# A ring of gathered rows with 24 slots instead of 32, in a two-layer graph network on one core

## The chip, the cores and the metric

The kernel runs on one core of a Trainium2 chip. The metric is the device time of one execution in microseconds (us). TensorE is called PE below, VectorE DVE, ScalarE ACT, GpSimd POOL and SyncE SP, as the profile does.

## The reference

The graph has 3125 nodes with 128 features and 53125 directed edges, sorted by their target node. The first network is three relational convolutions, the second a sum over neighbours with a small network behind it:

```python
def rgcn_conv(x, edge_index, edge_type, W, root, bias):
    out = x @ root + bias
    for r in range(8):
        mask = edge_type == r
        h = x @ W[r]
        msg = jnp.where(mask[:, None], h[src], 0)
        agg = segment_sum(msg, dst, N)
        cnt = segment_sum(mask, dst, N)
        out = out + agg / jnp.maximum(cnt, 1.0)[:, None]
    return out

h = relu(layernorm(x))
for W, root, b in three layers:
    h = relu(rgcn_conv(h, (src, dst), edge_type_8, W, root, b))
x = x + h
h = relu(layernorm(x))
h = h + segment_sum(h[src], dst, N)
h = relu(h @ W1 + b1) @ W2 + b2
x = x + batchnorm(h) * gamma + beta
```

## The kernel before

The edges are cut into 416 tiles of 128. A layer first makes a table in HBM: for each node its row times each of the eight relation matrices (`transform`, L512, on PE; `evacuate`, L742, on ACT and DVE; `store_rows`, L1073, on SP). Then, tile by tile, POOL gathers the 128 rows that a tile's edges name with one indirect DMA (`gather`, L1232, issued at L1234; the first 11 tiles of layers 1 and 2 at L1254, with their own indices). DVE writes a selection matrix of 128 by 64 for the tile (`select`, L946, the instruction at L958), which holds one over the edge count at each edge's target. PE multiplies the two and adds to the sums of a group of nodes in PSUM (`sum_tile`, L543, the matmul at L556). When the last tile of a group is summed, ACT closes it (`close_rel`, L750, the instruction at L752) and PE transforms its nodes for the next table.

There are three such layers (0, 1 and 2), so 1248 tiles in a row. The first 48 tiles of layer 0 (`FORE`) are gathered from the input instead, before the first table is ready (L1225), and don't use the ring. The other 1200 go through the ring `rows` of `SLOTS` slots. In what follows a **batch** is eight tiles (`BATCH`), counted from 0 at tile 48: layer 0 holds batches 0 to 45, layer 1 batches 46 to 97, layer 2 batches 98 to 149. The last tile of each layer comes by other DMAs, from SP (`fetch_ends`, L1088).

Beside the sums each layer has other work. In layer 0 DVE counts the edges of each key (L936, two instructions per tile). In layer 1 the neighbour matrix of the second network is built in 416 steps, one per tile, through all three engines: ACT makes a one-hot block (L840, L846), PE multiplies (`pairs`, L637), DVE adds it in place (`add`, L1046, the instruction at L1054). In layer 2 PE multiplies with that matrix (L663). At tile 12 of layers 1 and 2 (`LATE_SUM`) PE also runs `late_sums` (L601): 64 matmuls at L611 for the two last blocks of nodes, whose rows the first 11 gathers leave out.

The order on each engine is written out by hand, and engines meet at semaphores. Three rings tie the engines together:

- `rows`, `SLOTS` slots: POOL waits before each batch until PE has summed the batch that last used the slots. PE counts whole batches in `s_mm`.
- `sel`, 32 slots: DVE waits in the same way, also on `s_mm`, before each batch.
- each slot of `rows` has its own semaphore `s_row`, by which a gather tells PE that it has landed.

POOL's loop is this (L1247 to L1250):

```python
G = TILES * L + t
if G % BATCH == 0 and G >= FORE + SLOTS:
    pool.wait_ge(s_mm, (G + BATCH - SLOTS - FORE) // BATCH)
```

With 32 slots batch j waits until batches 0 to j-4 are summed. The space of `rows` is also used for some intermediate values before the first gather (L330 to L338), which need 2615 of its columns per partition.

Of the kernel before, what the change touches and what calls it, by code (L numbers as in the profile page):

```python
# [29 lines left out]
STEP = 7  # L30
EARLY = 32
HALO = 64
SLOTS = 32
BATCH = 8
SELS = 32
CHUNK = 16
# [51 lines left out]
def gnn_kernel(nc, x, src_t, dst_t, type_t, limits, w_rel, root_w, bias_w,  # L88
# [31 lines left out]
    def pieces(L, t):  # L120

        s, found = start_of[t], []
        for k, (b0, b1) in enumerate(span_of[L]):
            lo, hi = max(s, P * b0), min(s + SPAN, P * b1)
            if lo < hi:
                found.append((k, lo - P * b0, lo - s, hi - lo))
        return found
# [72 lines left out]
    def gathered(G):  # L200

        return sum(1 for g in range(FORE + (G - FORE) % SLOTS, G + 1, SLOTS) if g not in END_TILES)

# [17 lines left out]
    with ExitStack() as ctx:  # L221
        def sb(name, shape, dt=F32):
            return ctx.enter_context(nc.sbuf_tensor(name, shape, dt))

        def sem(name):
            return ctx.enter_context(nc.semaphore(name))

        x_rows = sb("x_rows", [P, BLOCKS, D])
        xT = sb("xT", [P, NP])
        rows = sb("rows", [P, SLOTS, D])  # L230
        sel = sb("sel", [P, SELS, SPAN])
# [175 lines left out]
        s_xT = sem("s_xT")  # L407
        s_row = [sem(f"s_row{n}") for n in range(SLOTS)]
        s_sel = sem("s_sel")
# [133 lines left out]
        def sum_tile(pe, L, t):  # L543
# [6 lines left out]
            else:  # L550
                pe.wait_ge(s_row[G % SLOTS], 16 * gathered(G))
                mine, edges = rows[:, G % SLOTS, :], slice(0, P)
            for k, at, in_window, width in pieces(L, t):
# [550 lines left out]
        def wait_table(pool, L):  # L1104
            if L == GIN:
                pool.wait_ge(s_xr_out, 16 * SUMS[LAST_REL])
                return
            for n in range(ALL_STAGES):
                pool.wait_ge(s_stage[n], 32 * stores_of(n, BLOCKS * (L + 1)))
# [101 lines left out]
        def _(pool):  # L1211
# [25 lines left out]
            with pool.If(fast != 0):  # L1237
                for L in range(GIN):
# [6 lines left out]
                    for t in range(0 if L else FORE, TILES):  # L1245
                        G = TILES * L + t
                        if L and t == LATE_TILES:  # L1247
                            wait_table(pool, L)
                        if G % BATCH == 0 and G >= FORE + SLOTS:
                            pool.wait_ge(s_mm, (G + BATCH - SLOTS - FORE) // BATCH)  # L1250
# [546 lines left out]
```

## Time and profile before

| | |
|---|---|
| median of three runs | 2008.41 us |
| all three | 2002.71, 2008.41, 2010.31 us |
| profiled execution, span from first to last instruction | 2002.7 us |
| profiled execution, its own time | 2002.71 us (the first of the three above: nothing lies around the span) |
| POOL busy | 1189.5 us, 59% |
| PE busy, matmuls | 1093.9 us, 55% |
| PE weight loads | 801.0 us, 40% |
| DVE busy | 848.6 us, 42% |
| ACT busy | 636.3 us, 32% |

A busy share says how long the engine's instructions are shown to run. POOL's instructions here are issues of indirect DMAs: what is shown is POOL's own part of them, not the transfer. "Idle before" in a row is the time that the engine sat idle before the instructions of the row; behind the arrow stands what ended it: "issue" is idle time with no wait that the profile shows, "remote" a semaphore whose writer the profile can't name.

### The profile page before, as it was taken

Reading aid. Unit: us, or ns where it says so; the run is one execution under the profiler, and the core shown is the slowest. Engines: PE = TensorE matmul, PEld = TensorE weight load, DVE = VectorE, ACT = ScalarE, POOL = GpSimd, SP = SyncE. Lnnn points to the kernel's source line nnn. Section 1 sums busy time; section 2 is a strip of 40 time slices with the busy share of each in tenths; the row PEclk is TensorE's granted clock in tenths of the full one; section 3 lists DMA queues with packets and bytes.
Section 4 is the critical chain, followed back from the end, with each engine's and each line's share of the span. In section 5 each row is a group of like instructions: output and inputs, shape, how many; then the busy total and the mean of one; then the engine's idle time right before and its main releaser. Section 6 shows DMA issues by size and latency. Waiting matters only on the chain.

```text
span 2002.7 us, 17513 instructions
## 1 busy us (share of the span) xinstructions
PE 1093.9 (55%) x4627; PEld 801.0 (40%) x4627; DVE 848.6 (42%) x3270; ACT 636.3 (32%) x1147; POOL 1189.5 (59%) x1254
## 2 busy tenths in 40 slices
PE   6496663344433454636564635584526445566677
PEld 2155343334333343434343424353524424253454
DVE  3365465565445235645655545562122212221223
ACT  4220410000000236756665656680201111111133
POOL 5445756666666555666566556645666666676650
PEclk8597866565556655656555565665557576666678
DMA  7352323242323311212222121222111111111111
GB/s 220 119 199 61 95 80 111 68 124 78 99 78 89 95 35 41 79 52 60 64 58 70 45 75 43 85 67 59 42 46 49 42 49 46 44 49 45 45 39 34
DMA packets 80801, 144.18 MB, mean 72 GB/s; under 512 B 24687, under 2 KB 38248, under 8 KB 80696
## 3 DMA queue, kind: packets, MB, share of 16 engines
q0 software_dynamic: 39840, 81.67, 15.9%
q1 hardware_dynamic: 40424, 60.68, 8.9%
q8 instruction: 41, 0.67, 0.1%
q10 hardware_dynamic: 432, 0.64, 0.1%
q14 instruction: 64, 0.52, 0.1%
HBM read 100.23 MB, written 42.67 MB: 71 GB/s over the span
## 4 chain that ended last, share of the span: by engine, by line
another core or an unknown queue 27%; PE 25%; issue 23%; DVE 20%; ACT 3%; SPq 1%; DMA 1%; DVEq 1%; ACTq 0%; POOLq 0%
PE ps_agg L556 8%; DVE sel L958 6%; DVE early L1054 5%; DVE agg_s L936 5%; PE ps_h L525 3%; PE ps_a L643 3%; DVE scratch L1043 2%; PE ps_h L663 2%; PE ps_a L663 2%; PE ps_a L574 2%; PE ps_agg L611 1%; PE ps_a L597 1%; ACT w_all L812 1%; PE ps_agg L585 1%
## 5 line engine op out<-in xcount | busy, mean ns | idle before, releaser
L1234 POOL DMA_INDIRECT rows<-h_table,idx x1175 | 1118.1, 952 | 683.3 <-issue 346.9
L556 PEld LDWEIGHTS ps_agg<-sel,rows 128*128 128x128 f32 x2764 | 570.9, 272 | 361.7 <-issue 335.0
L556 PE MATMUL ps_agg<-sel,rows 128*128 128x64 f32 (+14 forms) x2764 | 552.4, 332 | 254.6 <-issue 239.3
L958 DVE TENSOR_SCALAR sel<-iota,early,norm 128x64 f32<-128x64 f32 x1178 | 353.6, 333 | 432.9 <-remote 279.2
L643 PE MATMUL ps_a<-scratch 128*128 128x300 bf16 x416 | 162.0, 390 | 309.4 <-issue 150.0
L1054 DVE TENSOR_TENSOR early<-ps_a,early 128x300 f32 x416 | 195.9, 471 | 317.1 <-remote 254.1
L840 ACT ACTIVATE scratch<-scratch,ones 128x300 bf16<-128x300 f32 x416 | 221.3, 532 | 225.2 <-remote 198.0
L525 PE MATMUL ps_h<-w_all,xT 128*128 128x512 f32 x300 | 202.7, 787 | 111.1 <-issue 38.7
L846 ACT ACTIVATE scratch<-iota,code_lo 128x300 f32<-128x300 f32 x416 | 226.5, 545 | 12.5
L936 DVE TENSOR_SCALAR_CACHE_REDUCE agg_s<-scratch,key_f 128x256 bf16<-128x256 int16 x416 | 193.6, 473 | 50.1 <-issue 41.5
L643 PEld LDWEIGHTS ps_a<-scratch 128*128 128x128 bf16 x416 | 58.2, 140 | 351.0 <-issue 336.0
L1043 DVE TENSOR_SCALAR scratch<-iota,code_lo 128x128 bf16<-128x128 f32 x416 | 129.8, 312 | 0.0
L525 PEld LDWEIGHTS ps_h<-w_all,xT 128*128 128x128 f32 x300 | 63.0, 244 | 151.1 <-issue 73.9
L747 ACT COPY stage<-ps_h 128x512 f32<-128x512 f32 x80 | 46.4, 583 | 183.1 <-remote 111.4
L812 ACT CAST stage<-early 128x3072 bf16<-128x3072 uint8 x13 | 35.7, 2751 | 210.4 <-remote 117.8
L752 ACT ACTIVATE xT<-ps_agg,vecs 128x512 f32<-128x512 f32 (+2 forms) x16 | 9.4, 586 | 284.0 <-remote 246.4
L1225 POOL DMA_INDIRECT early<-x_table,early x48 | 45.9, 956 | 30.3 <-DMA x_table<-early 16.0
L663 PE MATMUL ps_h<-stage,scratch 128*128 128x512 bf16 x108 | 41.5, 496 | 21.5 <-issue 21.2
L812 ACT CAST w_all<-early 128x3072 bf16<-128x3072 uint8 x12 | 32.9, 2749 | 61.2 <-remote 45.4
L759 ACT ACTIVATE hid<-ps_agg,vecs 128x512 f32<-128x512 f32 (+3 forms) x10 | 5.3, 527 | 142.3 <-remote 102.9
L574 PE MATMUL ps_a<-early 128*128 128x384 f32 (+36 forms) x158 | 42.1, 397 | 11.5 <-issue 11.4
L936 DVE DVE_READ_ACCUMULATOR agg_s<-scratch,key_f 128x1 f32 x416 | 34.2, 82 | 31.4 <-issue 31.2
(157 smaller groups left out, 734.8 us busy)
## 6 DMA issues: line engine op xcount, KB each, us to landing
h_table<-stage SPq DMA_DIRECT2D x130, 256.0 KB
rows<-h_table,idx POOLq DMA_INDIRECT x1175
scratch<-key_rows SPq DMA_DIRECT2D x26, 544.0 KB
h_table<-scratch SPq DMA_DIRECT2D x20, 256.0 KB
x_rows<-in_x SPq DMA_DIRECT2D x6, 256.0 KB, 5.8
w_all<-in_W SPq DMA_DIRECT2D x3, 512.0 KB, 6.6
x_table<-early SPq DMA_DIRECT2D x6, 256.0 KB, 2.3
out<-early SPq DMA_DIRECT2D x6, 256.0 KB
```

Of the source, the lines that this page charges most:

```text
L525: nc.tensor.matmul(half_bank(L, b, half)[:], xT[:, block_of(b)], w_all[:, L, 4 * half:4 * half + 4, :].rearrange("p r o -> p (r o)"), star ...
L556: mm = nc.tensor.matmul(sums_of(L, k)[:, at:at + width], mine, sel[edges, G % SELS, in_window:in_window + width], start=False, stop=(t == ...
L643: nc.tensor.matmul(ps_a[a % A_BANKS][:, 0:HOT], low[:, a % HOTS, :], hot[:, a % HOTS, :], start=True, stop=True).then_inc(s_step, 1)
L663: mm = nc.tensor.matmul(ps_out[q][:], xp[:, b, part, :], fill_of(b)[:, WIDE * q:WIDE * q + WIDE], start=(b == 0 and part == 0), stop=False)
L812: nc.scalar.copy(fill_of(b), adjacency[:, b, 0:SPARE]).then_inc(s_fill, 1)
L840: nc.scalar.activation(hot[:, a % HOTS, :], apart[:, a % 2, :], ACT.Relu, bias=ones[:, 0:1], scale=-1.0).then_inc(s_hot, 1)
L846: nc.scalar.activation(apart[:, a % 2, :], iota[:, EARLY:EARLY + HOT], ACT.Abs, bias=code[:, a:a + 1]).then_inc(s_apart, 1)
L936: done = nc.vector.tensor_scalar(match[:, t % BATCH, :], chunks[:, c % 2, at:at + 2 * P], key_f[:, t:t + 1], 0.0, ALU.is_equal, ALU.add, a ...
L958: done = nc.vector.tensor_scalar(mine, here, dst, weight, ALU.is_equal, ALU.mult)
L1043: nc.vector.tensor_scalar(low[:, a % HOTS, :], iota[:, EARLY:EARLY + P], lo_f[:, a:a + 1], None, ALU.is_equal).then_inc(s_low, 1)
L1054: nc.vector.tensor_tensor(mine, ps_a[a % A_BANKS][:, 0:HOT].rearrange("p (b d) -> p b d", d=REACH), mine, ALU.add).then_inc(s_add, 1)
L1234: pool.indirect_dma_start(rows[:, slot, :], None, table, bass.IndirectOffsetOnAxis(ap=column, axis=0)).then_inc(landed, 16)
```

## The change

```diff
-SLOTS = 32
+SLOTS = 24
```

`SLOTS` is read in four places: the size of `rows` (24 slots of 512 bytes per partition, so 3072 columns, still more than the 2615), the number of `s_row` semaphores, the slot and the count that PE waits for in a tile (`G % SLOTS` and `gathered`), and POOL's wait. The wait stays one per batch, but with 24 slots batch j waits until batches 0 to **j-3** are summed, one batch more than before. Gathers, matmuls and all other instructions stay the same and in the same order.

On POOL this shows at one place, behind the wait for the first table, with the engine's waits shown. `s_mm` is the count of summed batches:

```order
 L1234 DMA rows<-h_table,idx 128x128 [waits s_stage3,s_stage2,s_stage4,s_stage1,s_stage0]
-L1234 DMA rows<-h_table,idx 128x128 x31
+L1234 DMA rows<-h_table,idx 128x128 x23
+L1234 DMA rows<-h_table,idx 128x128 [waits s_mm]
+L1234 DMA rows<-h_table,idx 128x128 x7
 L1234 DMA rows<-h_table,idx 128x128 [waits s_mm]
 L1234 DMA rows<-h_table,idx 128x128 x7
```

The first wait on PE comes after 24 gathers instead of 32, and from there on each wait asks for one batch more.

## Rows read from the trace of the kernel before

**Rows 1.** Groups of POOL's instructions: times, busy us, mean ns, idle before.

```profile
L1234 POOL DMA_INDIRECT rows<-h_table,idx x1175 | 1118.1, 952 | 683.3 <-issue 346.9 <-PE ps_agg L556 153.7 <-remote 144.8
```

**Rows 2.** Stretches of the first 48 gathers, busy us and instructions of each engine.

```profile
core 0: us, PE busy (x) PEld busy (x) DVE busy (x) ACT busy (x) POOL busy (x), PEclk, DMA share, GB/s
22.00:38.00 16.00, 15.95 (x44) 7.54 (x43) 4.67 (x6) 8.69 (x15) 12.14 (x13) 0.95 0.76 230
38.00:54.00 16.00, 4.98 (x6) 1.04 (x5) 0.09 (x1) 1.76 (x3) 12.04 (x14) 0.58 0.56 189
90.00:106.00 16.00, 14.51 (x35) 6.41 (x35) 11.97 (x51) 12.82 (x20) 0.00 (x0) 0.94 0.75 267
```

**Rows 3.** Timeline of POOL, layer 0: first gathers of batches 11, 28, 31, 33, 45.

```profile
259.17 1.15 POOL L1234 DMA_INDIRECT rows<-h_table,idx  x1 [7.80 <-PE ps_agg L556]
...
452.97 0.95 POOL L1234 DMA_INDIRECT rows<-h_table,idx  x1 [4.45 <-remote]
454.22 0.95 POOL L1234 DMA_INDIRECT rows<-h_table,idx  x1 [0.30 <-issue]
...
487.10 0.95 POOL L1234 DMA_INDIRECT rows<-h_table,idx  x1 [4.42 <-remote]
...
509.96 0.95 POOL L1234 DMA_INDIRECT rows<-h_table,idx  x1 [3.15 <-remote]
...
646.75 0.94 POOL L1234 DMA_INDIRECT rows<-h_table,idx  x1 [4.48 <-remote]
```

**Rows 4.** Stretches of batches 28 to 30, columns as in Rows 2.

```profile
453.00:467.00 14.00, 12.34 (x52) 11.39 (x52) 11.53 (x55) 0.00 (x0) 10.65 (x12) 0.50 0.32 89
467.00:487.00 20.00, 1.06 (x4) 0.86 (x3) 6.24 (x24) 0.00 (x0) 12.02 (x13) 0.50 0.18 46
```

**Rows 5.** Timeline: the last matmul of a group in layer 0, and ACT's closing.

```profile
374.66 0.17 PE L556 MATMUL ps_agg<-sel,rows 128*128 128x9 f32 x1 [2.42 <-issue]
...
395.95 0.69 ACT L752 ACTIVATE xT<-ps_agg,vecs 128x512 f32<-128x512 f32 x1 [63.68 <-remote]
```

**Rows 6.** Timeline of POOL, layer 1: first gathers of batches 46, 51, 53.

```profile
666.58 0.95 POOL L1254 DMA_INDIRECT rows<-h_table,late  x1 [11.39 <-issue]
...
733.64 0.97 POOL L1234 DMA_INDIRECT rows<-h_table,idx  x1 [17.24 <-PE ps_agg L556]
...
758.91 0.94 POOL L1234 DMA_INDIRECT rows<-h_table,idx  x1 [5.53 <-PE ps_agg L556]
```

**Rows 7.** Stretches at layer 1's start, as in Rows 2; half of `late_sums`, first to last start.

```profile
680.00:700.00 20.00, 2.25 (x9) 1.75 (x9) 2.67 (x9) 3.27 (x6) 15.12 (x17) 0.50 0.20 53
...
716.00:733.50 17.50, 16.82 (x78) 16.30 (x78) 4.10 (x15) 4.88 (x10) 0.39 (x1) 0.50 0.02 6
...
L611 PE MATMUL ps_agg<-w_all,stage x32: 275/402/447, 719.8 to 731.1; 128*128 128x64 f32 x16, 53*128 53x64 f32 x16
```

**Rows 8.** Timeline of POOL, layer 2: tile 11, then batches 103, 119, 146, and tile 414.

```profile
1356.92 0.95 POOL L1234 DMA_INDIRECT rows<-h_table,idx  x1 [2.10 <-issue]
...
1406.45 0.95 POOL L1234 DMA_INDIRECT rows<-h_table,idx  x1 [13.57 <-PE ps_agg L556]
...
1590.40 0.95 POOL L1234 DMA_INDIRECT rows<-h_table,idx  x1 [6.68 <-PE ps_agg L556]
...
1898.94 0.95 POOL L1234 DMA_INDIRECT rows<-h_table,idx  x1 [4.41 <-remote]
...
1942.04 0.94 POOL L1234 DMA_INDIRECT rows<-h_table,idx  x1 [0.30 <-issue]
```

**Rows 9.** The stretch of `late_sums` in layer 2, columns as in Rows 2.

```profile
1371.00:1396.00 25.00, 3.44 (x12) 3.43 (x12) 1.93 (x8) 0.00 (x0) 16.70 (x18) 0.50 0.19 50
```

**Rows 10.** Timeline of POOL, layer 1: first gathers of batches 59, 60, 62.

```profile
832.31 0.95 POOL L1234 DMA_INDIRECT rows<-h_table,idx  x1 [1.98 <-remote]
...
843.95 0.95 POOL L1234 DMA_INDIRECT rows<-h_table,idx  x1 [1.94 <-remote]
...
869.86 0.94 POOL L1234 DMA_INDIRECT rows<-h_table,idx  x1 [6.13 <-PE ps_agg L556]
```

## The prediction

> **What bounds the kernel now.** I read four views in this order: the groups of POOL's instructions, the stretches, POOL's timeline, and PE's and ACT's timelines beside it. In the groups the reader sees POOL, with 1175 of the 1197 ring gathers on one line, busy 1118.1 us, idle 683.3 us before them, and a good half of that "issue" [rows 1]. A gather takes 0.95 us and the next starts 1.25 us after it, so eight seem to take 10.0 us [rows 3]. That isn't the real pace. From batch 11 to batch 45 the starts move by 646.75 - 259.17 = 387.6 us for 34 batches, 11.40 us each: 34.13 us for three (28 to 31), 22.86 us for two (31 to 33) [rows 3]. The pauses of 4.4 us after three batches and 3.15 us after two are what the 1.25 us pace left out. So a gather really costs about 34.13 / 24 = **1.42 us**, and a pause only brings POOL's shown time level with its real time. In layer 2 it is the same: batches 119 to 146 take (1898.94 - 1590.40) / 27 = 11.43 us each [rows 8]. 1197 gathers of 1.42 us are 1700 us of the 2002.7. POOL is the bound of layers 0 and 2, and what it loses outside this are true waits.
>
> The second thing to see is what a long run of gathers does to everyone else. POOL issues its first 48 gathers without a pause from 22 us on. In the first 16 us PE starts 44 matmuls and ACT 15 instructions; in the next 16 us PE starts 6, DVE 1 and ACT 3. After 90 us, when 48 real gathers (68 us) are over, the counts are 35, 51 and 20 again [rows 2]. The same in layer 0: in the 14 us behind the pause at 452.97 PE starts 52 matmuls and DVE 55 instructions, in the 20 us after that 4 and 24, though POOL issues as before; the pause at 487.10 ends it [rows 3, 4]. Signals are late too: the last matmul of a group starts at 374.66, but ACT's closing starts at 395.95, just before POOL's next run [rows 5]. I call this a **slow stretch**. In these rows it begins about 14 to 16 us after POOL's last restart and ends when POOL has to stop and its real work is done. A longer ring lets POOL run on for longer between stops, so it buys rows in advance and pays with slow stretches.
>
> **The change, part by part.** No instruction is added or removed. Batch j now waits for batch j-3 instead of j-4: each stop comes one batch earlier, 8 x 1.42 = 11.4 us of real work.
>
> *Layer 0, start.* POOL truly waits for PE here (7.80 us idle before batch 11 [rows 3]; 1.42 x 8 - 10.0 = 1.4 us of it for each batch run without a pause is only levelling). A slot less asks for a batch that comes up to 11.4 us later, and the slow stretch before it ends up to 11.4 us earlier. I take 0, with both ends, -11.4 and +11.4.
>
> *Layers 0 and 2, steady.* POOL stays at its real pace. PE's rows come up to 11.4 us later, covered by PE's distance behind POOL. If that cover is gone PE waits for each gather, and still POOL sets the pace. What is new is more stops: 11.43 us per batch in runs of two against 11.38 in runs of three; in runs of one it is 843.95 - 832.31 = 11.64 [rows 10]. Over 34 batches in layer 0 and 43 in layer 2 (103 to 146) that is 77 x 0.05 = 4 us if three become two, and 77 x 0.26 = 20 us if all become one. Three became two is what one batch less makes, so +4.
>
> *Layer 0, end.* Batch 46 starts at 666.58 [rows 6], 19.8 us after batch 45, which has seven gathers (its tile 415 comes by SP): 7 x 1.42 = 9.9 us of work and 9.9 us of waiting for the table, whose last transforms PE does in the burst after the slow stretch that ended at 646.75. A slow stretch one batch shorter lets PE reach them earlier, at most by the 9.9 us; nothing makes them later but rows that come late. I take -4, ends -9.9 and 0.
>
> *Layer 1, start.* This is the largest term. POOL runs through batches 46 to 50 (40 gathers) and then waits 17.24 us for batch 47, until 733.64 [rows 6]. In batch 47 lies `late_sums`. Between 680 and 700 PE starts 9 matmuls in 20 us; between 716 and 733.5 it starts 78 in 17.5 us, `late_sums` among them, at the same granted clock of 0.50 (the 1.2 GHz level) [rows 7]. With 24 slots POOL must stop after 24 gathers, at 666.58 + 24 x 1.42 = 700.7, wait for batch 46 (summed by then), and run batch 49 alone before it has to wait for batch 47. From 700.7 on PE finds only 11.4 us of gathers, less than the 14 us at which stretches turned slow. PE had still to do one or two tiles (about 1 us each when quick) before the point it was at by 716: it gets there at 702.3, and finishes batch 47 17.6 us later (733.64 - 716), at 719.9 instead of 733.6: **-13.7**. POOL's batch 51, which now asks for batch 48, is not late by this. Layer 1 behind that point is paced by PE, DVE and ACT, not by POOL's pace (batches 53 to 62 take (869.86 - 758.91) / 9 = 12.3 us each [rows 6, 10]), so I let the gain stand to the layer's end. Within layer 1 each gather batch is released by PE already; released by j-3 instead of j-4 the same pattern runs one batch apart, and I take 0. The ends of the term are 0 (the signal of batch 46 comes late, nothing is won) and -16.
>
> *Layer 2, start.* The same form, but POOL is the bound behind it. From 1356.92 POOL runs 29 gathers, to the end of batch 102, real end 1398.1; PE starts 12 matmuls in the 25 us from 1371 to 1396 [rows 9], and batch 103 waits for batch 99 until 1406.45 [rows 8]. With 24 slots POOL stops after 21 gathers, at 1386.7. PE is quick 11.4 us earlier, less some 1.7 us for what it did in them anyway: batch 99 is done at 1396.7. Batch 102 starts then, 103 at 1408.1: **+1.6**, ends -2 and +11.4 (the full batch, if the slow stretch doesn't shorten). If a stop before 1590.40 then goes away, where POOL truly waits 6.68 - 3 x 1.4 = 2.4 us, that wait is late next and I leave it.
>
> *End.* The last gather starts at 1942.04 [rows 8], 60 us before the end, and PE has over two batches to sum behind it; with a shorter ring it can't be that far behind. Up to -8, taken as 0, since PE's dense work there has to be done in any case.
>
> Sum: 0 + 4 - 4 - 13.7 + 0 + 1.6 + 0 = -12.1 us. It stands against the profiled execution, 2002.7, which is also the fastest of the three; against the median, 2008.4, it gives **1996 us**.
>
> **The rivals.** *A, slower: the lost batch isn't paid back.* Its place is the stop behind which POOL is the bound: the start of layer 0 and batch 103. If slow stretches follow the number of gathers in flight or some clock of their own and don't shorten, each costs the full 11.4 us, 22.8 in all, and the more frequent stops cost 4 to 20 more: 2008.4 + 27 = 2035, up to 2051. It decides from the point at which batch 103 starts later than about 1412 on the clock of before. For it speaks that POOL is the bound; against it the three places [rows 2, 4, 7] where the slowness begins after a run of POOL and ends with it. The Trainium skill's page "DMA: Bandwidth & Descriptors" has in its "Rules for kernel authors" the rule to issue a DMA early and wait on its semaphore late, since its fixed cost is then hidden; by it 32 slots are the better ring, and this rival is what it would do. The trace speaks half against it: beyond about 14 us the early issue slows those who need the rows.
>
> *B, no difference.* The 13.7 us at layer 1's start are given back, because layer 1's pace isn't PE's own but set by the same slow stretches, which there depend on how PE and POOL fall together (11.64 us for one batch, 25.9 for the next two [rows 10]). Then 0 + 4 + 0 + 1.6 - 4 = 2010.
>
> *C, much faster.* The opposite in layer 1: the pattern with its double runs turns into single runs of 11.64. Layer 1's 44 batches from 53 on would win up to 44 x (12.3 - 11.6) = 31 us more: 1965.
>
> That the change does nothing because the ring never fills is excluded: POOL's stops are the ring's stops.
>
> **How the numbers follow.** A measurement of this kernel can tell about 0.5% from no change, here 10 us. My forecast has 0.45, with a range of its own of 1980 to 2010: the bounds of its terms added as if they were independent. B has 0.24, A 0.22, C 0.09. Faster than 1998.4 are two thirds of the forecast's cases, C, and a sixth of B: 0.30 + 0.09 + 0.04, and I give 0.44. Slower than 2018.4 are nearly all of A, a tenth of B and little of the forecast: 0.24. The rest, 0.32, is no difference. The range from 1970 to 2037 leaves out the far half of A and of C, about 0.15 to 0.2.
>
> **What would show it.** POOL's first wait for PE comes after 24 ring gathers, and runs between pauses are mostly of two batches. The pause of 17.24 us in layer 1 becomes two, and PE's `late_sums` there begins some 13 us earlier after the layer's first gather. In layer 2 batch 102, not 103, is the one that waits long, and 103 starts within 3 us of where it did, counted from the layer's first gather. The steady pace stays at 11.4 to 11.5 us per batch. I am wrong if slow stretches begin as early and last as long as before, if the steady pace goes over 11.7, or if layer 1's batches take more than 12.5 us each.

## The result, and the profile after

The changed kernel takes **1986.36 us** (median of 11 runs, 1970.03 to 2004.73), the kernel before, run beside it, 2010.31 us (11 runs, 1999.54 to 2034.9). The ratio is 0.9856, 95% interval [0.9829, 0.9883]: 1.4% faster, some 29 us. It leaves out slow runs, those over 1.5% above their kernel's fastest (three of the changed kernel's eleven), while the medians of all runs are 24 us, 1.2%, apart. Forecast were 1996 us and 0.6%. The time lies in the range, but the gain is at least twice the one forecast, and the sum's largest error has one place, the end of the program.

The page of the changed kernel: span, busy time, and the groups that answer to [rows 1] and to PE's sums.

```profile
span 1980.7 us, 17490 instructions
...
PE 1113.7 (56%) x4604; PEld 815.1 (41%) x4627; DVE 848.9 (43%) x3270; ACT 635.1 (32%) x1147; POOL 1187.1 (60%) x1254
...
L1234 POOL DMA_INDIRECT rows<-h_table,idx x1175 | 1115.8, 950 | 688.7 <-issue 343.3
...
L556 PE MATMUL ps_agg<-sel,rows 128*128 128x64 f32 (+14 forms) x2764 | 582.5, 341 | 255.7 <-issue 193.4
```

Nothing is to be seen in these totals: POOL is as busy and as idle as in [rows 1], within 6 us. The gain must be found in the order of time. POOL's timeline after, where it restarts: a steady stop in layer 0, the first gathers of layer 1 (batch 46), a pause inside batch 47, batch 51, the first gather of layer 2 (batch 98), batch 102, and the last gather.

```profile
333.30 0.94 POOL L1234 DMA_INDIRECT rows<-h_table,idx  x1 [4.75 <-remote]
...
670.38 0.94 POOL L1254 DMA_INDIRECT rows<-h_table,late  x1 [9.38 <-issue]
...
687.15 0.97 POOL L1234 DMA_INDIRECT rows<-h_table,idx  x1 [3.34 <-issue]
...
726.74 0.97 POOL L1234 DMA_INDIRECT rows<-h_table,idx  x1 [13.62 <-PE ps_agg L556]
...
1329.66 0.94 POOL L1254 DMA_INDIRECT rows<-h_table,late  x1 [12.09 <-DMA h_table<-stage]
...
1382.82 0.94 POOL L1234 DMA_INDIRECT rows<-h_table,idx  x1 [10.53 <-PE ps_agg L556]
...
1934.38 0.94 POOL L1234 DMA_INDIRECT rows<-h_table,idx  x1 [0.31 <-issue]
```

Counted from layer 1's first gather, the long wait of layer 1 ends 56.4 us later (726.74 - 670.38), where it was 67.1 us ([rows 6]: 733.64 - 666.58). Both waits are for the same sum, that of batch 47: batch 50 asks for it now, batch 51 did before. The stretches that answer to [rows 2], [rows 7] and [rows 9], and half of `late_sums`:

```profile
core 0: us, PE busy (x) PEld busy (x) DVE busy (x) ACT busy (x) POOL busy (x), PEclk, DMA share, GB/s
...
38.00:54.00 16.00, 5.21 (x6) 1.29 (x6) 0.00 (x0) 1.75 (x3) 12.15 (x13) 0.59 0.56 183
...
684.00:704.00 20.00, 13.35 (x59) 11.89 (x59) 10.10 (x42) 10.32 (x21) 12.88 (x14) 0.63 0.24 67
704.00:727.00 23.00, 11.98 (x54) 11.84 (x55) 4.70 (x16) 5.10 (x10) 7.24 (x9) 0.50 0.10 24
1361.00:1383.00 22.00, 10.63 (x45) 10.11 (x44) 0.41 (x2) 1.84 (x1) 8.73 (x11) 0.50 0.12 31
...
L611 PE MATMUL ps_agg<-w_all,stage x32: 275/401/467, 702.0 to 724.2; 128*128 128x64 f32 x16, 53*128 53x64 f32 x16
```

In layer 1 PE starts 59 matmuls in the 20 us from 684 on, where [rows 7] had 9, and in layer 2 45 in the 22 us up to batch 102's start, where [rows 9] had 12 in 25. `late_sums` starts 31.6 us after the layer's first gather (702.0 - 670.38) instead of 53.2 (719.8 - 666.58), but runs for 22.2 us instead of 11.3, so its head start is not all kept. The slow stretch within the first 48 gathers, which the ring doesn't touch, is unchanged.

The last lines of the sums, by PE's timeline: first the kernel before, then after. The last gather starts at 1942.04 before [rows 8] and at 1934.38 after.

```profile
1968.44 0.43 PE L556 MATMUL ps_agg<-sel,wide 5*128 5x64 f32 x2
```

```profile
1945.20 0.43 PE L556 MATMUL ps_agg<-sel,wide 5*128 5x64 f32 x2
```

PE's last sum followed POOL's last gather by 26 us before and by 11 us now. This **tail** is the part of the gain that the prediction put at nothing.

### The profile page after: what moved, and what is told of

It is laid out like the page before. It is cut to its first block, busy times and chain, and to the rows that moved or that the text cites. A ratio compares the mean times of both kernels' runs of the same rounds, so it can differ in the third digit from the quotient of the medians.

```text
span 1980.7 us, 17490 instructions
## 1 busy us (share of the span) xinstructions
PE 1113.7 (56%) x4604; PEld 815.1 (41%) x4627; DVE 848.9 (43%) x3270; ACT 635.1 (32%) x1147; POOL 1187.1 (60%) x1254
## 4 chain that ended last, share of the span: by engine, by line
issue 23%; PE 20%; POOL 20%; another core or an unknown queue 19%; DVE 12%; ACT 3%; DMA 1%; SPq 1%; DVEq 1%; ACTq 0%; POOLq 0%
POOL rows L1234 20%; PE ps_agg L556 5%; DVE early L1054 5%; PE ps_a L643 3%; DVE sel L958 3%; PE ps_h L525 3%; DVE scratch L1043 2%; PE ps_a L574 2%; PE ps_agg L611 1%; PE ps_a L663 1%; ACT scratch L840 1%; PE ps_h L663 1%; DMA rows<-h_table,idx 1%; PE ps_a L597 1%
## 5 line engine op out<-in xcount | busy, mean ns | idle before, releaser
L556 PEld LDWEIGHTS ps_agg<-sel,rows 128*128 128x128 f32 x2764 | 585.4, 276 | 381.2 <-issue 297.2
L556 PE MATMUL ps_agg<-sel,rows 128*128 128x64 f32 (+14 forms) x2764 | 582.5, 341 | 255.7 <-issue 193.4
L747 DVE COPY stage<-ps_h 128x512 f32<-128x512 f32 x50 | 34.0, 680 | 37.8 <-remote 16.6
```

The costliest lines, as they stand in the source:

```text
L556: mm = nc.tensor.matmul(sums_of(L, k)[:, at:at + width], mine, sel[edges, G % SELS, in_window:in_window + width], start=False, stop=(t == ...
L747: copy(stage_of(H)[:, 512 * half:512 * half + 512], half_bank(L, b, half)[:]).then_inc((s_evA, s_evD)[half], 1)
```

## The experiments

There were eighteen runs, some of them of the same kernel again, in five groups, each group on one chip beside the kernel before. The chips turned out to be of two kinds, and this matters more than any edit. On the one kind (two chips, called **A chips** here, and by its time the chip of the first result) the kernel before takes 2007 and 2012 us; on the other (three chips, **B chips**) it takes 1622 us. Each result below says which kind it is from. "j-3" means that a batch waits for the one three before it.

### The wait alone

32 slots, waits as in the changed kernel:

```diff
-if G % BATCH == 0 and G >= FORE + SLOTS:
-    pool.wait_ge(s_mm, (G + BATCH - SLOTS - FORE) // BATCH)
+if G % BATCH == 0 and G >= FORE + 24:
+    pool.wait_ge(s_mm, (G + BATCH - 24 - FORE) // BATCH)
```

> The ring keeps its 32 slots; only POOL's wait asks for batch j-3 instead of j-4. Theory (a shorter run of gathers gives shorter slow stretches, the slots themselves do nothing): as the changed kernel, ratio to before 0.982 to 0.990, layer 1's long wait for PE split in two, PE's last sum 12 to 20 us earlier. Rival (the smaller ring itself, its addresses or its 8 semaphores fewer, brings the time): 0.997 to 1.003.

A chip: 1983.63 us (1976.76 to 1992.91), ratio 0.9882 [0.9826, 0.9938], the same as the changed kernel within the intervals. It is the wait that brings the gain; the ring's size and its place in memory have no part in it that can be seen.

### One batch less again

The same edit with 16 in place of 24, so j-2.

> 32 slots, but POOL's wait asks for batch j-2, as a ring of 16 would. Theory: nearly every run of gathers is one batch, so slow stretches almost vanish, but now PE lacks rows: a batch takes 11.4 us of gathers and 2.2 us to land, while PE is left with one batch in hand. Layers 0 and 2 stay at 11.6 to 11.8 us per batch (some +20 us against the changed kernel), layer 1 gets 0 to +2 us per batch: 1990 to 2080 us, slower than the changed kernel. Rival (the shorter the run the better): under 1965 us.

A chip: 1969.24 us (1958.42 to 1974.92), ratio 0.9777 [0.972, 0.9834]. I had expected it to be slower or equal, and it is the fastest kernel on this kind of chip. PE's group now says why it isn't better still: its idle time ends mostly with a row that lands, so PE runs right behind the gathers.

```profile
L556 PE MATMUL ps_agg<-sel,rows 128*128 128x64 f32 (+14 forms) x2764 | 656.2, 359 | 291.5 <-DMA rows<-h_table,idx 208.1
```

### Gathers paced by their landing

As before (j-4), but each gather first waits until that two before it has landed:

```diff
+back = G - 2 - ((G - 2) in END_TILES)
+if G not in END_TILES and back >= FORE:
+    pool.wait_ge(s_row[back % SLOTS], 16 * gathered(back))
```

> As before, 32 slots and batch j-4, but each gather also waits until the gather two places before it has landed, so POOL can't run ahead of its real work. Theory in its strong form (slow stretches come from gathers that POOL has issued and not really done): they vanish, PE starts over 40 matmuls in every stretch of 14 us of layer 0, a gather is shown to start every 1.4 to 1.45 us, and the time falls by 40 to 110 us (1900 to 1970), since layer 1's PE, DVE and ACT are quick all the time. Rival (slow stretches belong to the real work of gathers, whoever waits): slow stretches as before, 2000 to 2060 us, the upper end by the added waits.

A chip: 1990.35 us (1989.24 to 1994.4), ratio 0.9898 [0.9847, 0.9949]. Stretches of layer 0 in this kernel, and then the same stretches in the kernel before:

```profile
450.00:470.00 20.00, 8.66 (x26) 6.44 (x26) 6.97 (x34) 0.00 (x0) 12.11 (x13) 0.50 0.25 71
470.00:490.00 20.00, 11.99 (x41) 9.49 (x41) 10.06 (x48) 0.00 (x0) 11.55 (x13) 0.50 0.24 68
490.00:510.00 20.00, 15.29 (x37) 9.37 (x38) 6.50 (x29) 1.86 (x3) 12.95 (x14) 0.50 0.29 85
```

```profile
450.00:470.00 20.00, 13.60 (x56) 12.37 (x56) 14.45 (x68) 0.00 (x0) 13.07 (x14) 0.50 0.26 72
470.00:490.00 20.00, 2.05 (x4) 1.39 (x5) 7.29 (x29) 0.69 (x1) 11.92 (x14) 0.50 0.23 67
490.00:510.00 20.00, 12.57 (x47) 8.39 (x45) 8.64 (x39) 1.32 (x3) 12.88 (x15) 0.67 0.30 89
```

With at most two gathers under way none of these stretches falls to 4 matmuls; with the free run one does, and bursts of 56 stand beside it. So the collapse depends on gathers handed over in advance. But the time falls by 17 us, not by the 40 to 110 of the expectation, because the pacing isn't free: batches 11 to 45 take 427.9 instead of 387.6 us, while layer 1 takes 632.2 instead of 674.8 and the tail is 4 us.

### One place at a time

j-3 in some batches only, j-4 in the others; the edit names them:

```diff
-if G % BATCH == 0 and G >= FORE + SLOTS:
-    pool.wait_ge(s_mm, (G + BATCH - SLOTS - FORE) // BATCH)
+if G % BATCH == 0:
+    j = (G - FORE) // BATCH
+    back = j - (3 if 46 <= j < 52 else 4)
+    if back >= 0:
+        pool.wait_ge(s_mm, back + 1)
```

> As before, but batches 46 to 51 alone (the start of layer 1) wait for j-3. Theory: the term of layer 1's start alone, -10 to -14 us (ratio 0.993 to 0.996), the matmuls of late_sums in layer 1 start 10 to 14 us earlier after the layer's first gather, and the rest as before. Rival (the gain of the change is spread evenly over all stops): -1 us, 0.998 to 1.001.

A chip, batches 46 to 51 alone: 2004.62 us (1999.42 to 2016.46), ratio 0.9984 [0.9956, 1.0012]. The place on which the prediction's largest term stands brings 3 us by itself (interval -2 to 9), not 13.7. The wait there does end early (at 727.84, by POOL's timeline, 52 us after the layer's first gather instead of 67), and the trace shows where it is lost again. PE is done with batch 47 14.6 us earlier than in the mean of three traces with j-4 in all of layer 1, but with batch 49 only 4.7 us earlier and with batch 60 4.1. From 727.84 on POOL, soon back on the longer wait, runs three batches without a stop, where j-3 throughout runs two, and batch 49 is summed only behind that run.

Batches 140 to 149 alone, on an A chip (`j` from 140 to 149 in the edit above):

> 32 slots, j-3 for batches 140 to 149 only. On a chip with slow stretches (before about 2007 us): theory 1 (the end is a gain of its own) ratio 0.993, PE's last sum 11 to 15 us behind POOL's last gather instead of 26.6; theory 2 (POOL's last gather comes as much later as the tail gets shorter) 0.998 to 1.002. On a chip without them: 1.000, as in the two runs before.

2009.65 us (1993.82 to 2022.46), ratio 0.998 [0.9946, 1.0015]. POOL's last gather and PE's last sum:

```profile
1961.73 0.94 POOL L1234 DMA_INDIRECT rows<-h_table,idx  x1 [0.30 <-issue]
```

```profile
1976.37 0.43 PE L556 MATMUL ps_agg<-sel,wide 5*128 5x64 f32 x2
```

The tail shrinks to 14.6 us, as theory 1 said. But the last gather comes 611.7 us after the layer's first, where the other kernels with j-4 in layer 2 have 600.7 to 606.7 (table below), and the ratio is theory 2's. Most of this delay lies ahead of the edit, though. Batch 135 is still under the old wait; its first gather starts here, first line, and in the kernel before, second line:

```profile
1788.38 0.94 POOL L1234 DMA_INDIRECT rows<-h_table,idx  x1 [3.31 <-remote]
```

```profile
1773.19 0.95 POOL L1234 DMA_INDIRECT rows<-h_table,idx  x1 [3.26 <-remote]
```

From there the last gather follows after 173.4 us here and after 168.8 to 171.8 in three traces with j-4, so POOL pays about 3 us; PE's last sum follows after 188.4 instead of 195.7 to 199.6, about 9 us earlier. The truth by this trace lies between the theories, nearer to theory 1. The timed runs (-4 us, interval -11 to 3) neither show these 9 us nor exclude them; theory 1's 0.993 lies just outside their interval.

The same kernel and those with j-3 in whole layers fell on B chips:

> 32 slots, and POOL waits for batch j-3 only in the last ten batches (140 to 149), for j-4 everywhere else. Theory 1 (the end is a gain of its own: with one batch less bought in advance the last slow stretch is shorter, and PE, which only starts to sum at full pace when POOL's real work is over, has less left): PE's last sum follows POOL's last gather by about 11 to 15 us instead of 26.6, POOL's last gather keeps its place, the time is 0.993 of the kernel before (about -12 us of 2007). Theory 2 (the gain behind the last gather only answers to how far POOL is ahead, and the total is POOL's and PE's common pace): POOL's last gather starts as many us later as the tail gets shorter, ratio 0.998 to 1.002.

> 32 slots, j-3 in layers 0 and 2, j-4 in layer 1. If the parts of the result simply add up, as the shifts in the trace of the changed kernel say: first gather of layer 1 up to 4 us later than before, layer 1 unchanged, then layer 2's own -10 us (its last sum against its first gather): about -8 us, ratio 0.996. If all of the gain comes at the end of layer 2 whatever is before it: -12 to -15, ratio 0.993. If shorter runs of gathers only pay when all layers have them: 1.000.

> 32 slots, j-3 in the whole of layer 1, j-4 in layers 0 and 2. Theory 1 (parts add, and within layer 1 the gain lasts only if the shorter distance holds through the layer): layer 2's first gather comes 15 us earlier after layer 1's first one than before (675 to about 660 us), and the end of the program keeps its 26.6 us behind the last gather: ratio 0.992 to 0.993. Theory 2 (layer 1 has a pace that doesn't depend on the distance, and the layer's start is given back as in the run with batches 46 to 51 alone): layer 1 lasts 673 to 677 us, ratio 0.999 to 1.001.

> 32 slots, j-3 for batches 140 to 149 only, once more. First sort of chip: theory 1 (the end is a gain of its own) 0.993, with PE's last sum 11 to 15 us behind POOL's last gather instead of 26.6; theory 2 (POOL's last gather starts as much later as the tail gets shorter) 0.998 to 1.002. Second sort: 1.000, as at first.

> 32 slots, j-3 in the whole of layer 1 only, once more. First sort of chip: theory 1 (the gain lasts if the shorter wait holds through the layer) layer 1 lasts 660 instead of 675 us, ratio 0.992 to 0.993; theory 2 (it is given back as in the run with batches 46 to 51 alone) 0.999 to 1.001. Second sort: 1.000, as at first.

> 32 slots, j-3 in layer 1 only. On a chip with slow stretches: if the 1.4% is the sum of parts, layer 1 lasts 10 to 15 us less (from its first gather to layer 2's), and the ratio is 0.992 to 0.995. If layer 1's gain is given back as with batches 46 to 51 alone: 0.998 to 1.001. On a chip without them: 1.000 to 1.001, as twice before.

> 32 slots, j-3 in layers 0 and 2, j-4 in layer 1. On a chip with slow stretches: POOL's last gather is followed by PE's last sum after about 11 to 15 us instead of 26.6. If that is a gain because the batch of lead that POOL gives up is given up where POOL waits anyway (layer 2's start) and not in the steady part (as with the last ten batches alone, where POOL lost 11 us and the tail won 12): the last sum comes 10 to 15 us earlier after layer 2's first gather than before (627 us), ratio 0.992 to 0.995. If not: 0.998 to 1.002. On a chip without them: 1.001, as before.

| B chip | median us | ratio |
|---|---|---|
| last ten batches | 1622.7 | 1.0004 [0.9994, 1.0013] |
| again | 1623.73 | 1.0012 [1.0002, 1.0021] |
| layers 0 and 2 | 1623.68 | 1.0008 [0.9998, 1.0018] |
| again | 1623.65 | 1.0008 [0.9998, 1.0018] |
| layer 1 | 1622.7 | 1.0004 [0.9994, 1.0013] |
| twice more | 1623.25, 1622.99 | 1.0011 [1.0001, 1.002], 1.0004 [0.9994, 1.0013] |

Seven misses as far as the question goes (none of them times a whole layer's share on an A chip), and one finding: on these chips there is no gain to be placed.

### What is different on a B chip

The first 48 gathers stand in every kernel in the same form. These are the stretches of [rows 2] on a B chip, in the kernel with j-3 in the last ten batches:

```profile
22.00:38.00 16.00, 16.00 (x44) 7.42 (x42) 4.66 (x6) 8.68 (x15) 11.72 (x13) 0.95 0.72 219
38.00:54.00 16.00, 13.85 (x36) 5.64 (x36) 14.05 (x70) 11.76 (x18) 12.24 (x13) 1.00 1.05 381
```

In the first 16 us the two kinds of chip agree to the instruction: 44 matmuls, 6 on DVE, 15 on ACT. In the next 16 us the A chip starts 6, 1 and 3 [rows 2], this one 36, 70 and 18, while POOL's gathers look alike on both (13 or 14 of them). The DMAs, too, move only half as much on the A chip in those 16 us, 189 against 381 GB/s. **The slow stretches belong to the A chips.** POOL's steady gathers on this B chip:

```profile
452.30 0.95 POOL L1234 DMA_INDIRECT rows<-h_table,idx  x1 [0.30 <-issue]
453.55 0.94 POOL L1234 DMA_INDIRECT rows<-h_table,idx  x1 [0.30 <-issue]
454.80 0.94 POOL L1234 DMA_INDIRECT rows<-h_table,idx  x1 [0.30 <-issue]
456.05 0.94 POOL L1234 DMA_INDIRECT rows<-h_table,idx  x1 [0.30 <-issue]
...
L1234 POOL DMA_INDIRECT rows<-h_table,idx x1175 | 1114.3, 948 | 358.1 <-issue 358.1
```

The same 1.25 us from start to start, but here without a pause: all idle time is the 0.30 us between gathers, and 34 batches (11 to 45) take 339.7 us, 9.99 each, where the A chip has 11.40. The ring never fills on this chip, with 24 slots no more than with 32, so the edit has nothing to act on. The 1.42 us per gather is an A chip's figure.

### Shorter waits where nothing is slow

The changed kernel again, j-2 again, and a wait before the *fifth* gather of a batch until the batch before it is summed, which leaves 12 gathers in advance:

```diff
-if G % BATCH == 0 and G >= FORE + SLOTS:
-    pool.wait_ge(s_mm, (G + BATCH - SLOTS - FORE) // BATCH)
+if G % BATCH == 4 and G >= FORE + 12:
+    pool.wait_ge(s_mm, (G + 4 - BATCH - FORE) // BATCH)
```

> The changed kernel itself, once more. Eight runs so far fell into two sorts: on one chip the kernel before took 2007 us, POOL's gathers had real costs of 1.42 us and slow stretches stood behind long runs of them; on another it took 1622.6 us, gathers followed one another every 1.25 us for over 300 us without a pause and no slow stretch is to be seen. If the chip here is of the first sort (before over 1950): ratio 0.983 to 0.989 as at first. If it is of the second (before under 1700): with no slow stretch there is nothing to win. POOL is then the bound nearly everywhere and the j-3 of layers 0 and 2 alone gave 1.0008, so 1.0005 to 1.002. A theory in which the gain comes from the order of the work and not from slow stretches says under 0.995 there too.

> 32 slots, waits for j-2, once more. First sort of chip (before over 1950): ratio 0.972 to 0.984 as at first. Second sort (before under 1700): slower than before, since a wait for four gathers more than in the run with 12 in advance (1.0248 there) still covers landing and sums in the steady parts, but not the layers' starts: 1.002 to 1.015. If slow stretches are the whole cause of the gain, no kernel with a shorter wait is faster on a chip without them.

> 32 slots; POOL waits before the fifth gather of each batch j until batch j-1 is summed, so at that point 12 gathers are ahead of the sums, where the kernel with j-2 has 16. Theory 1 (slow stretches are what costs, every batch less in advance saves some at the layers' starts and at the end, and the pace of layers 0 and 2 is POOL's 11.4 us per batch as long as PE has its rows before POOL needs the signal): the pace stays under 11.6, the time is 1950 to 1970, ratio 0.97 to 0.98. Theory 2 (with four gathers less the signal of the sum comes after POOL's real work is over: landing of the last row, some matmuls and the signal take longer than the 5.7 us that four gathers cover): every batch loses 1 to 3 us, the pace is 12 to 14 us per batch, the time 2020 to 2250.

| in advance | A chip | B chip |
|---|---|---|
| 24 (j-3) | 0.9856 [0.9829, 0.9883] | 1.0008 [0.9999, 1.0018] |
| 16 (j-2) | 0.9777 [0.972, 0.9834] | 1.0152 [1.0135, 1.0169] |
| 12 | not run | 1.0248 [1.0231, 1.0265] |

On B chips the order is turned round. POOL's group of the j-2 kernel and of the one with 12, on B chips, show where it goes, waits for PE, which the kernels with 32 or 24 in advance don't have:

```profile
L1234 POOL DMA_INDIRECT rows<-h_table,idx x1175 | 1115.2, 949 | 383.2 <-issue 356.2 <-PE ps_agg L556 27.0
```

```profile
L1234 POOL DMA_INDIRECT rows<-h_table,idx x1175 | 1113.5, 948 | 399.0 <-issue 355.6 <-PE ps_agg L556 43.4
```

With j-2 these waits lie at the layers' starts: layer 0 lasts 472.5 us instead of 461.0 (from the ring's first gather to layer 1's), layer 1 526.5 instead of 519.0, and layer 2 up to batch 103 56.9 instead of 49.9, together 26 us, against 25.1 us in the times (1646.96 - 1621.88). The steady pace is 10.0 us per batch with 32, 24, 16 and 12 alike. My expectation of 1.002 to 1.015 for j-2 was just short; that for 12, which gave either 0.97 to 0.98 or 2020 us and more, was made for an A chip and says nothing of this one.

The Trainium skill's page "DMA: Bandwidth & Descriptors" has in its "Rules for kernel authors" the rule to issue a DMA early and to wait on its semaphore late. The two columns answer it differently. On the B chips 16 and 12 in advance, which issue later, are 1.5% and 2.5% slower, as the rule has it (24 is no different from 32); on the A chip the rule fails, by 2.2% for 16 gathers against 32.

### Is it POOL's surplus of gathers?

If slow stretches come from gathers handed over every 1.25 us and worked off every 1.42 us, handing them over more slowly should end them. One small POOL instruction behind each ring gather (the lines that set up its buffer and its semaphore are left out here):

```diff
+n = next(paused)
+if n >= 2:
+    pool.wait_ge(s_pause, n - 1)
+nc.gpsimd.iota(pause[:, n % 2, :], pattern=[[1, 4]], base=0, channel_multiplier=0
+               ).then_inc(s_pause, 1)
```

> The kernel before (32 slots, j-4) with one small POOL instruction (an IOTA of 128x4) behind each ring gather, so that POOL hands over its gathers at some 1.42 to 1.55 us instead of 1.25 us (the IOTA of 128x48 has 0.20 us on the page; the gap between two of POOL's instructions comes on top). On a chip where gathers follow one another every 1.25 us for hundreds of microseconds (before about 1622 us) this prices the pace alone: 1197 gathers by 0.17 to 0.30 us, 1825 to 1980 us, ratio 1.125 to 1.22. On a chip with levelling pauses and slow stretches (before about 2007 us): theory 1, slow stretches come from gathers handed over faster than they are worked off (1.25 against 1.42 us), so without a surplus there are none: POOL's pace becomes 1.42 to 1.55 us without pauses, nothing else is late, 1850 to 1980 us, ratio 0.92 to 0.985. Theory 2, slow stretches have another cause: the pauses stay, each gather costs the more: 2050 to 2200, ratio 1.02 to 1.10.

A chip: 2020.87 us (2008.68 to 2028.88), ratio 1.0035 [1.0, 1.007]. POOL's timeline says that it didn't test what it was made for:

```profile
450.58 0.95 POOL L1237 DMA_INDIRECT rows<-h_table,idx  x1 [0.17 <-issue]
451.54 0.14 POOL L1265 IOTA pause<- 128x4 int32 x1
451.85 0.94 POOL L1237 DMA_INDIRECT rows<-h_table,idx  x1 [0.17 <-issue]
...
460.88 0.95 POOL L1237 DMA_INDIRECT rows<-h_table,idx  x1 [4.13 <-remote]
```

The 0.30 us between gathers became 0.14 of IOTA and 0.17 of gap: 1.27 us from start to start instead of 1.25, and the pauses are still there. What shows as idle "issue" between gathers has room for a small instruction at almost no cost.

The changed kernel with the same instruction:

> The changed kernel (24 slots, j-3) with the same small POOL instruction behind each ring gather. If slow stretches are what the shorter ring saves, and the instruction takes them away (or there are none on this chip), the two padded kernels agree within 0.5% of each other. If the shorter ring's gain is from something else, this one is 1% or more faster than the padded kernel with 32 slots.

A chip: 2002.91 us (1994.8 to 2021.28), ratio 0.996 [0.9925, 0.9995] to the kernel before, so about 0.9% under the other padded one (2002.91 / 2020.87). It repeats the sign of the change on a second A chip.

Two IOTAs (128x2) behind each gather:

> The kernel before (32 slots, j-4) with two small IOTAs behind each ring gather. With one, the idle time between gathers shrank from 0.30 to 0.17 us and took most of it in, so the gathers only went from 1.25 to 1.27 us apart, less than the 1.42 us at which they are worked off; with two they should be 1.42 to 1.48 us apart. On a chip with slow stretches: theory 1 (slow stretches come from a surplus of gathers handed over) they are gone or short, the levelling pauses are gone, 1850 to 1960 us, ratio 0.92 to 0.98. Theory 2 (they come from the work on the gathers itself, whatever POOL's surplus) PE, DVE and ACT stay as slow behind runs of gathers, 2005 to 2080 us, ratio 1.00 to 1.035. On a chip without them (before 1622 us) the pace alone is priced: 1197 gathers by 0.17 to 0.23 us, 1825 to 1900 us, ratio 1.125 to 1.17.

B chip: 1758.77 us (1755.84 to 1759.93), ratio 1.0839 [1.082, 1.0857], so it is no test of the surplus, but it prices the pace:

```profile
450.47 0.96 POOL L1237 DMA_INDIRECT rows<-h_table,idx  x1 [0.16 <-issue]
451.43 0.30 POOL L1266 IOTA pause<- 128x2 int32 x2
451.83 0.97 POOL L1237 DMA_INDIRECT rows<-h_table,idx  x1
...
455.92 0.96 POOL L1237 DMA_INDIRECT rows<-h_table,idx  x1 [0.16 <-issue]
```

Gathers start (455.92 - 450.47) / 4 = 1.363 us apart, 0.114 more than 1.249; times 1197 that is 136 us, and the time rose by 1758.77 - 1622.1 = 136.7. On a B chip POOL's pace is the kernel's, one for one. A pace of 1.42 alone would by this cost 1197 x 0.17 = 203 us and give an estimated 1825 us. The A chips take 2007. By this estimate some 180 us of their time are not POOL's pace but waits: the slow stretches' price, of which j-3 gets 24 to 29 us back and j-2 38 to 45 (by the medians and by the ratios).

## Why the prediction was right or wrong

Single traces of the same instructions differ on an A chip by 10 us and more in a layer (layer 0 in four traces with j-4: 546.3 to 559.2 us). So I compare all traces of A chips, in us from first gather to first gather; "tail" is from POOL's last gather to PE's last matmul over gathered rows (the second of the pair in the rows above, 0.2 us later than the first). Three chips stand in this table, and each row is one execution.

| waits (traces) | layer 0 | layer 1 | layer 2 | tail |
|---|---|---|---|---|
| j-4: before | 546.3 | 674.8 | 600.7 | 26.6 |
| j-4: padded | 554.8 | 671.3 | 606.1 | 27.9 |
| j-3 in 46 to 51 | 554.0 | 658.8 | 606.7 | 27.6 |
| j-3 in 140 to 149 | 559.2 | 665.9 | 611.7 | 14.8 |
| j-3: after | 548.7 | 659.3 | 604.7 | 11.0 |
| j-3: wait alone | 550.7 | 649.3 | 603.9 | 14.4 |
| j-3: padded | 551.9 | 659.0 | 609.4 | 15.5 |
| j-2 | 548.3 | 650.2 | 605.8 | 8.8 |

Means with j-4 (each column over the rows that have it there) against j-3 throughout: layer 0 553.6 and 550.4, layer 1 670.7 and 655.9, layer 2 to the last gather 604.5 and 606.0, tail 27.3 and 13.6. The differences, -3.2 - 14.8 + 1.5 - 13.7 = -30.2 us, stand against 29 by the ratio and 24 by the medians; with traces that scatter by 10 us in a layer, so close an agreement is in part luck.

- *Layer 0* (0, half of +4, and -4): right; -3 is within the traces' scatter.
- *Layers 0 and 2, steady* (+4 in all): right in size. Batches 11 to 45 take 387.6 to 394.8 us with j-4 and 389.7 to 392.4 with j-3, 11.5 us per batch. In layer 2, from 119 to 146, a batch takes 11.43 to 11.68 us with j-4 and 11.65 to 11.76 with j-3, at the 11.7 that the prediction named as a sign of being wrong, though the layer as a whole is only 1.5 us longer. But "Three became two is what one batch less makes" was wrong: after the change runs between stops are of one to four batches (378.75 to the next stop at 401.98 is two, 436.42 to 482.15 is four).
- *Layer 1* (-13.7): the size is right, and so, by the traces, is the step at its start. PE is done with batch 47 52.4 to 56.1 us after the layer's first gather with j-3, 65.9 to 67.3 with j-4, in the mean 12.9 us earlier, and the lead stays: 12.4 us at batch 60, 12.6 at batch 70, 14.9 at batch 97. So the gain is made at the layer's start. That it stood by itself ("I let the gain stand to the layer's end") was too much: the shorter wait has to go on. With it in batches 46 to 51 only, 4.1 of 14.6 us are left at batch 60, and the timed runs won 0.16% [-0.12, 0.44] where the term asks for 0.7%. (That trace ends the layer 11.9 us early all the same; behind batch 51 its waits are those of the kernel before, so I take this for scatter.)
- *Layer 2's start* (+1.6): right within the 3 us that the prediction allowed. Batch 102, not 103, waits long (10.53 us, at 1382.82), and 103 starts 63.2 us after the layer's first gather against 65.1.
- *The end* (0, bound -8): **this is the step that failed.** "Up to -8, taken as 0, since PE's dense work there has to be done in any case." It measures -13.7, beyond its own bound, and is about half of the gain. The paragraph on layer 2's start holds the contradiction: if batch 103 starts at the same time as before but needs one batch more to be summed, PE is a batch of 11.4 us further on at the same time. As POOL's pace is the same behind it, PE stays that much closer, and is done that much earlier behind the last gather. I booked the batch where it is given up, and not where it comes back. The traces show it on its way. With j-3 PE is done with batch 112 186.7 to 193.7 us after layer 2's first gather, with j-4 (the kernel before, the padded one and the one with the last ten batches) 201.2 to 206.6: 12.7 us earlier in the mean, while POOL's first gather of batch 112 moves by 0.4 us. The run with the last ten batches shows the same from the other end: one batch less of lead there brings PE's last sum some 9 us forward and costs POOL about 3.

With -13.7 in place of 0 the sum would have been -25.8, 1983 us.

*The rivals.* A (slower, the lost batch isn't paid back) falls on A chips: its deciding point, batch 103 past 1412 on the clock of before, isn't reached (63.2 us after layer 2's first gather, which is 1404.6 on that clock). B chips are nearly its picture for shorter waits: with no slow stretch to shorten, j-2 costs 1.5%. B (no difference) is right only on the chips that it wasn't made for, though what it describes, a gain of the start that is given back, is what the run with only batches 46 to 51 does. C (layer 1 in single runs) isn't what is seen: its runs stay mixed.

*The slow stretch itself* was read rightly in its course: it begins after a run of POOL and ends when POOL stops, a shorter lead shortens it (59 matmuls for 9 at layer 1's start), gathers paced by landing break it up. That it is a property of the chip I couldn't see in one trace, and didn't ask.

*The pauses* I read too simply. "A pause only brings POOL's shown time level with its real time": its length does go with the number of gathers before it, but each of these pauses is a wait for PE's count `s_mm`, and what is late is the signal. The stop at 487.10 in the kernel before (4.42 us [rows 3]) waits for batch 27. PE has long summed it; these are PE's last matmul before POOL's restart and its next one:

```profile
472.78 0.27 PE L556 MATMUL ps_agg<-sel,rows 128*128 128x64 f32 x1 [1.84 <-issue]
488.48 1.22 PE L525 MATMUL ps_h<-w_all,xT 128*128 128x512 f32 x1 [15.44 <-ACT xT L752]
```

So the count that lets POOL go at 487.10 comes from a matmul that ended 14 us before or earlier; by PE's order it ended 25.8 us before. Of the 71 pauses over 0.9 us in this trace POOL restarts in 68 within 0.3 us of a recorded update of `s_mm`, and in 46 the matmul behind the awaited count had ended before POOL even stopped. On a B chip the five such pauses of the j-2 kernel all end 0.27 us behind the matmul. The 1.42 us are therefore the pace at which an A chip gets through gathers and signals together; that they are POOL's own work is not shown. The steady pace of the sum, and so its terms, don't depend on which of the two it is.

**Open**: what makes a chip an A chip, and what holds its signals back; whether handing gathers over at 1.42 us ends the slow stretches (one IOTA was too short, two fell on a B chip); and, in timed runs on an A chip, what each layer's share is. A ring of 40 slots wasn't tried.

**The best version** depends on the chip: j-2 on A chips (1969 us in four runs on one chip, under both kernels), the kernel before or the changed one on B chips (1622 and 1624 us). The changed kernel is the safe one of the three: 1.4% gained on the one kind, 0.1% (at most 0.2%) lost on the other.

## What to carry to other kernels

A lead of one engine over another is an account: when a ring is made shorter, look where the lead is given up (nearly free here at layer 2's start, where POOL waited anyway) and book its return at the end, where the follower has that much less left. More in advance has no value of its own: in this kernel 24 gathers did as well as 32 on the B chips, and on the A chips, where long runs of gathers slow the other engines, fewer was better. When a pause ends, look up when the instruction behind the awaited count ended: a late signal looks like a slow engine. And before a gain of 1% is believed, time it on a second chip: here j-2 wins 2.2% on one kind and loses 1.5% on the other.

## What the runs showed of the hardware

- Two kinds of chips under one kernel: 2007 and 2012 us against three times 1622 us, with all but the same durations of single instructions (a gather shown with 0.95 us on both, DVE's selection matrix with 333 and 334 ns in the pages of the kernel before and of a B chip's run).
- The difference begins only about 16 us into a run of back-to-back gathers: from 22 to 38 us the counts are identical, from 38 to 54 us the A chip has a sixth of the matmuls (6 against 36), 1 of DVE's instructions against 70 and half of the GB/s (189 against 381).
- A shown duration can hide this wholly. On both kinds a gather is 0.95 us and the next follows at 1.25; on the A chip eight take 11.4 us in the mean, and only the pauses after one to four batches say so.
- On the A chip signals come late behind runs of gathers: at POOL's pauses in the kernel before, the restart is 4.8 us (median), at most 31.9 us, behind the end of the matmul whose count it waits for. On a B chip (j-2) it is 0.27 us at all five pauses.
- Where the profile shows 0.30 us "issue" between two gathers, a 0.14 us IOTA in it costs 0.02 us (measured on an A chip); the second one costs about 0.09 (on a B chip).
